# Softmax of a 16-head attention: exponentials of the scores read in place, one instruction a head

## What is computed

```python
Q = proj(q, wq_w, wq_b); K = proj(k, wk_w, wk_b); V = proj(v, wv_w, wv_b)   # 16 heads of 16
scores = jnp.einsum('bhqd,bhkd->bhqk', Q, K) / jnp.sqrt(jnp.float32(D_K))
scores = jnp.where(mask == 0, jnp.float32(1e-09), scores)
attn = jax.nn.softmax(scores, axis=-1)
out = jnp.einsum('bhqk,bhkd->bhqd', attn, V)
...
return out @ wo_w.T + wo_b
```

## Time and profile before

| what | us |
|---|---|
| median of 3 runs | 1713.43 (1711.95 to 1716.44) |
| the profiled execution, its own time | 1717.48 |
| its span in the trace | 1715.8 |
| TensorE (matrix products) busy | 1318.1 |
| VectorE busy | 1207.6 |
| ScalarE busy | 820.5 |
| GpSimd busy | 513.5 |

### The profile page before, as it was taken

The page is one execution under the profiler, slowest core; times in us unless marked ns, Lnnn a source line. Parts: engine busy times, 40 slices in busy tenths (PEclk is TensorE's granted clock), DMA queues, the critical chain, the costliest instruction groups (busy, mean ns, idle before and its releaser), DMA issues. The chain is left out here.

```text
span 1715.8 us, 31957 instructions
## 1 busy us (share of the span) xinstructions
PE 1318.1 (77%) x10558; PEld 1074.2 (63%) x10559; DVE 1207.6 (70%) x2061; ACT 820.5 (48%) x1218; POOL 513.5 (30%) x589
## 2 busy tenths in 40 slices
PE   6169999999997619999068998999999079761077
PEld 3159888888896318888047787788878045320066
DVE  3869755665664569965077888888886877898944
ACT  3447433333332317633045555555554046886764
POOL 0055666666553024664212223322221000000000
PEclk9579999999999759999568888888887579996599
DMA  9457433333322556632420000000000100235311
GB/s 321 155 157 218 97 54 53 50 50 47 50 41 28 176 176 184 188 54 33 84 86 10 11 9 9 9 9 9 12 7 1 55 1 1 110 132 220 125 44 56
DMA packets 103445, 134.31 MB, mean 78 GB/s; under 512 B 16192, under 2 KB 87488, under 8 KB 101568
## 3 DMA queue, kind: packets, MB, share of 16 engines
q1 hardware_dynamic: 81856, 103.33, 18.3%
q0 software_dynamic: 21504, 29.83, 10.8%
HBM read 88.43 MB, written 44.70 MB: 78 GB/s over the span
## 5 line engine op out<-in xcount | busy, mean ns | idle before, releaser
L600 ACT ACTIVATE top_x_all<-top_h_ps,top_b1T 128x256 f32<-128x256 f32 x448 | 186.3, 473 | 322.0 <-PE top_h_ps L480 268.8
L478 PE MATMUL top_h_ps<-top_xT_hi,top_w_hi 128*128 128x256 f16 x896 | 246.8, 275 | 1.9 <-DVE top_xT_lo L779 1.0
L479 PE MATMUL top_h_ps<-top_xT_lo,top_w_hi 128*128 128x256 f16 x896 | 246.7, 275 | 0.0
L480 PE MATMUL top_h_ps<-top_xT_hi,top_w_lo 128*128 128x256 f16 x896 | 246.7, 275 | 0.0
L496 PE MATMUL top_y_ps<-top_w_hi,top_x_all 128*128 x896 | 244.5, 273 | 0.0
L497 PE MATMUL top_y_ps<-top_w_lo,top_x_all 128*128 x896 | 244.4, 273 | 0.0
L498 PE MATMUL top_y_ps<-top_w_hi,top_x_all 128*128 x896 | 244.4, 273 | 0.0
L358 POOL DMA_INDIRECT x_sum<-top_x_all,top_rows_out x112 | 188.7, 1685 | 123.4 <-POOL top_rows_out L354 73.9
L790 DVE CAST top_x_all<-top_x_all 128x512 f16<-128x512 f32 x224 | 99.1, 442 | 149.8 <-ACT top_x_all L600 135.5
L792 DVE TENSOR_TENSOR top_x_all<-top_x_all 128x512 f16<-128x512 f32 x224 | 155.7, 695 | 7.7
L346 POOL DMA_INDIRECT top_xg<-normed,top_rows_in x112 | 121.7, 1086 | 90.1 <-POOL top_rows_in L343 81.0
(11 more groups left out here) (293 smaller groups left out, 3133.8 us busy)
## 6 DMA issues: line engine op xcount, KB each, us to landing
top_staged<-in_L_xattn_W SPq DMA_DIRECT2D x32, 512.0 KB
top_staged<-in_L_ffn_w SPq DMA_DIRECT2D x32, 512.0 KB
up_raw<-ffn_u_all SPq DMA_DIRECT2D x48, 256.0 KB, 2.1
ffn_yT<-up_raw SPq DMA_DIRECT2D x12, 1024.0 KB, 4.8
normed<-top_x_all SPq DMA_DIRECT2D x2, 4096.0 KB, 14.1
top_w_lo<-in_ctx SPq DMA_DIRECT2D x4, 1024.0 KB, 9.9
top_x_all<-in_x SPq DMA_DIRECT2D x4, 1024.0 KB, 11.9
x_sum<-top_x_all SPq DMA_DIRECT2D x4, 1024.0 KB, 11.5
```

The costliest lines, as they stand in the source:

```text
L478: nc.tensor.matmul(out, hi, xT_hi[p][:, c, :], start=(c == 0), stop=False)
L479: nc.tensor.matmul(out, hi, xT_lo[p][:, c, :], start=False, stop=False)
L480: last = nc.tensor.matmul(out, lo, xT_hi[p][:, c, :], start=False, stop=(c == DC - 1))
L600: last = nc.scalar.activation(h32[:, fc * R:(fc + 1) * R], h_ps[:, b, q * R:(q + 1) * R], ACT.Relu, bias=b1T[:, bass.ds(e * FC + fc, 1)], ...
```

## The change

`softmax_shift` is taken out, on VectorE, for both halves, and its semaphores with it. VectorE takes the maximum with its sign turned (`negate=True`), and before it does so it waits for the exponentials of the same half of the batch before, which read `top`. ScalarE's `exps` waits for that maximum and for the transposes of the batch before, and then runs one instruction a head, 8 for a half: each reads 128 scores a partition from PSUM, adds the negated maximum as the bias (one value a partition, from `top` in SBUF) and writes the exponentials to `prob`. The positions of `exps` in ScalarE's list stay as they are.

```diff
             def exps(m, p, i, r):
-                this(act, s_sub[r], m, p)
-                part = prob[:, r * HC:(r + 1) * HC, :]
-                A.activation(part, part, ACT.Exp).then_inc(s_exp[r][p], 1)
+                this(act, s_top[r], m, p)
+
+                last(act, s_pt[r], m, p)
+                for c in range(HC):
+                    h = r * HC + c
+                    mm = A.activation(prob[:, h, :], S[:, r, c, :], ACT.Exp, bias=top[:, h:h + 1])
+                mm.then_inc(s_exp[r][p], 1)
...
                 this(dve, s_mask[r], m, p)
-                V.tensor_reduce(top[:, r * HC:(r + 1) * HC], S[:, r], AX_X, ALU.max).then_inc(s_top[r][p], 1)
-
-            def softmax_shift(m, p, i, r):
-                this(dve, s_top[r], m, p)
-
-                last(dve, s_pt[r], m, p)
-                V.tensor_tensor(prob[:, r * HC:(r + 1) * HC, :], S[:, r],
-                                top[:, r * HC:(r + 1) * HC].unsqueeze(2).to_broadcast(wide), ALU.subtract).then_inc(s_sub[r][p], 1)
+                last(dve, s_exp[r], m, p)
+                V.tensor_reduce(top[:, r * HC:(r + 1) * HC], S[:, r], AX_X, ALU.max, negate=True).then_inc(s_top[r][p], 1)
...
                 on(front_bias, 1)
-                on(softmax_shift, 0, 0)
                 on(out_low, -2)
                 on(value_bias, 1)
                 on(softmax_top, 0, 1)
                 on(finish, -2)
-                on(softmax_shift, 0, 1)
                 on(divide, -1)
```

More of the change, by code:

```diff
@@ L917, in attention @@
         s_top = [two(f"top{r}") for r in range(2)]; s_mask = [two(f"masked{r}") for r in range(2)]
-        s_sub = [two(f"shifted{r}") for r in range(2)]; s_exp = [two(f"exp{r}") for r in range(2)]
+        s_exp = [two(f"exp{r}") for r in range(2)]
         s_pt = [two(f"prob_transposed{r}") for r in range(2)]; s_pT = [two(f"probT{r}_ready") for r in range(2)]
```

## The result

The changed kernel takes 1744.8 us (median of 4 runs, 1741.4 to 1748.2) against 1714.9 us for the kernel before on the same chip: a ratio of 1.0176, 95% interval 1.0148 to 1.0205. It is slower by 30 us. The forecast was 1752 us, in a range from 1719 to 1792.

The account below looks back on a forecast made before the run. No engine is full; a lap of 13.64 us a slot through TensorE, ScalarE and VectorE bounds it. Adding 0.72 and 1.14 gives 15.50, less 0.5 is 15.0; over 28 slots 38 us are lost: 1752 us, range 1719 to 1792.

Parts of the forecast that it names:

- The lap, not the busy times: Attention: no engine is full; a chain through TensorE, ScalarE and VectorE, 13.64 us a slot in five pieces, sets the time.
- 2.19 us for eight exponentials: ScalarE, each half: seven starts 0.26 us apart and 0.37 us for the last, in place of 1.06 us.
- Half 0: +0.72, half 1: +1.14: Microseconds added a slot: bias of Q to half 0's transposes 3.01 to 3.73; copy of Q to `front_in` 2.77 to 3.91.
- The subtraction of half 1 earns nothing: VectorE: this 1.22 us subtraction is off the lap, so removing it gains no time.
- the slow stretch: TensorE's clock at 0.50 for 3.41 us after its wait for half 0's exponentials, costing 1.67 us of the lap.
- the first piece: Lap from TensorE's transposes of half 0's exponentials to ScalarE's copy of Q, 3.89 us.
- TensorE waits near 2 us and near 1 us: Sign expected in the new trace: waits ahead of the transposes of half 0 and of half 1, respectively.
- take off 0.5: Allowance, in us a slot, for the slow stretch partly leaving the lap: 15.50 becomes 15.0.
- the slow stretch at other places than said: Named sign of a wrong prediction: TensorE's half-speed clock falling elsewhere than on the lap's first piece.
- Rival 1: TensorE's clock also falls after its wait ahead of half 1's transposes: slot 16.7 us, 1800 us, chance 0.12.
- the second piece: Lap from ScalarE's copy of Q to its `front_in` copy: 2.77 us, forecast 3.91, about 5.1 at slow clock.
- Rival 2: Slow stretch wholly beside the lap and exponential steps a little quicker than 0.26 us: no change, 1713 us, chance 0.06.

Follow-up runs that it names:

- half 0 alone: The change made only for half 0, half 1 keeping its subtraction and single exponential, with 24 unused products a slot on TensorE: 1691.3 us, ratio 0.989.
- single: Changed kernel with one exponential of 1024 a half and one maximum a row over its 8 heads as bias: 1694.3 us; with 16 unused products a slot 1651.9 us.
- half 1 alone: The change made only for half 1, half 0 keeping its subtraction and single exponential, with 24 unused products a slot on TensorE: 1727.7 us, ratio 1.012.
- early0_fill: Changed kernel with half 0's exponentials ahead of the splits of Q and K, plus 10 unused products a slot on TensorE: 1714.6 us, ratio 1.000.

## Why the prediction was right, point by point

- *The lap, not the busy times.* Right: 82 us less work on VectorE bought nothing. The lap of five pieces holds to 0.02 us at full clock (13.83 against 13.81).
- *2.19 us for eight exponentials.* Right: 2.16 to 2.18. The pace by which I worked it out from the 256-column row was 0.26 us; one slot's row has 2.00 us over eight starts, 0.25. The value of the Trainium skill, page "ScalarE: Activation LUTs", section "What ACT_TABLE_LOAD costs", came to 0.294 us a start; with 0.387 us for the last the estimate from that page is 7 x 0.294 + 0.387 = 2.45 us, and the trace has 0.28 less.
- *Half 0: +0.72, half 1: +1.14.* Shown apart at full clock: 12.67 is 0.70 over the 11.97 that I had worked out, and 13.10 is 1.13 over it. With both, 13.80 is 1.83 over it, where I had 1.86 (15.50 less 13.64).
- *The subtraction of half 1 earns nothing.* Right with the slow stretch in the first piece: there it ends 0.82 us before the exponential of half 1 starts. Not at full clock: there it holds that exponential by 0.2 us, and the measured lap of before is 12.19 us, not 11.97.
- *TensorE waits near 2 us and near 1 us.* Right: 1.93 and 0.87.
- *The slow stretch: the step that was off.* The prediction says: "the wait ahead of the first piece, which the slow stretch follows now, grows (to about 2.1 us), so I leave most of it on the path and take off 0.5: 15.0 us". The wait grew, and yet in 18 of 24 slots no slow stretch followed it. In the other six it lasted 10.23 us and cost 2.88. The mean is 14.52 us a slot, so what was to be taken off is 15.50 - 14.52 = 0.98 us, not 0.5. Over 28 slots this is 13 us too much. The measured runs lie 7 us below the forecast. The 0.5 was a guess that no row gave, and no steady slot takes the 15 us that it made, so that the time came out this near is partly luck. The prediction had named "the slow stretch at other places than said" as a sign of being wrong, and by that sign its account of the clock was wrong; that of the lap was right.
- *Rival 1, a second slow stretch.* Its mechanism is real and its price for the second piece was right (5.1 us, measured 5.12), but it comes in a quarter of the slots and not in all. That its slot of 16.7 us met the measured 16.68 is luck: it had the slow clock on the whole first piece (3.89 us) and none on the last (3.73), and the rows have 2.92 and 4.50.
- *Rival 2, no change.* It had a chance of 0.06, and both of its conditions nearly held in 18 of 24 slots: no slow stretch on the lap, and steps of 0.25 us (it asked for 0.247). Those slots are only 0.16 us over the old ones, of 0.88 us in the mean; the rest of the loss stands in the other six.
- *What came back.* With the clock held up the laps differ by 1.60 us a slot, 45 us over 28 slots. The kernel before pays 13.64 - 12.19 = 1.45 us a slot for the slow clock and the changed one 14.52 - 13.80 = 0.72 on average, so 20 us come back and 25 are left. A reader of the two totals alone would have put the change at little more than half its price.

What stays open is why the clock follows a wait of 1.13 us each time in one kernel and a wait of 1.93 us one time in four in the other. With products in the wait ahead of half 0 the clock is 0.99 or 1.00 in four kernels (both of the case, half 0 alone, `single`), but 0.92 with half 1 alone and 0.89 in `early0_fill`. The rows give no rule for it.

## What to carry to other kernels

Follow the lap of a software pipeline through the engines before counting busy time: a pass taken from VectorE is worth only what the lap waits for it, and work put on ScalarE costs double where two of its places lie on the lap. Splitting one instruction of 1024 columns in eight costs seven starts, here 1.1 us; where a wider bias will do (one maximum over all heads of a row instead of one a head) the pass goes and the starts don't come. That form needs scores of one row that lie close enough over the heads: a head whose largest score is some 80 or more below that of its neighbours would lose all its exponentials. And price TensorE's clock apart from the lap, since a change that moves waits moves the slow stretches too. Filling the waits with products that nobody reads does it, if the profile then shows the clock near 1.00; where it does not, the products stand ahead of real work and add their own time.

## What the runs showed that I had not expected

- Products without any use made the kernel before faster by 2.1% (1671.9 against 1709.2 us), and they made the form with one exponential a half 2.4 points faster (0.964 against 0.988).
- The clock stayed at 1.00 past a wait of 1.93 us in three slots of four; once at 0.50 it stayed there through 10.23 us in which TensorE was busy without a break. In the kernel before, a stretch of 3.41 us at 0.50 came once in each slot of 13.64.
- Where GpSimd's sum of two tensors and VectorE's masked copy meet, the one that began second is slow and the first is not: the sum takes 1.16 us when it began first and 2.13 behind the masked copy, and the masked copy 2.08 behind a sum against 1.23 alone. An order in ScalarE's list that put the split of K second made TensorE wait 1.2 to 1.3 us in the slots shown.
